# One attention kernel, eight batches: the last query projection a unit later, picks around the first scores, one key stack on GpSimd's queue

## The reference

```python
h = relu(layernorm(x))
q, k, v = h @ Wq.T + bq, h @ Wk.T + bk, h @ Wv.T + bv      # split into 8 heads of 32
scores = einsum('bhqd,bhkd->bhqk', q, k) * 32 ** -0.5
scores = scores * (adj + adj)[:, None]                     # 1024 x 1024 per head
attn = softmax(scores, axis=-1)
x = x + einsum('bhqk,bhkd->bhqd', attn, v) @ Wo.T + bo
```

## Time and profile before

| | us |
|---|---|
| median of 3 runs (lowest to highest) | 3013.35 (3013.23 to 3013.98) |
| the profiled execution's own time | 3014.05 |
| its span, first to last instruction | 3012.2 |
| TensorE matmuls busy | 2938.3 (98%) |
| VectorE busy | 1873.0 (62%) |
| ScalarE busy | 1492.1 (50%) |
| GpSimd busy | 702.0 (23%) |

### The profile page before, as it was taken

One profiled execution on the slowest core, in us unless ns is written; L12 is line 12 of the kernel. 1 busy time (PEld: TensorE's weight loads), 2 busy tenths in 40 slices (PEclk: granted clock), 3 DMA queues, 4 the chain that ended last, 5 costly groups with the idle time before them and its releaser, 6 DMA issues.

```text
span 3012.2 us, 63662 instructions
## 1 busy us (share of the span) xinstructions
PE 2938.3 (98%) x23040; PEld 2370.1 (79%) x23040; DVE 1873.0 (62%) x4154; ACT 1492.1 (50%) x2761; POOL 702.0 (23%) x1273
## 2 busy tenths in 40 slices
PE   7999999999999999999999999999999999999999
PEld 6787787877878778788787887888868888688886
DVE  2798427984278742787428874288643886438863
ACT  1784217833178332782328732287323873238722
POOL 0343003430034201242013420134201341013410
PEclk9999999999999999999999999999999999999999
DMA  5202212022120221202311113111121112220200
GB/s 173 92 2 92 78 71 92 2 92 79 70 92 2 92 106 52 84 14 80 132 36 73 41 53 133 48 59 58 56 113 70 38 70 68 89 81 26 82 8 14
DMA packets 96344, 204.34 MB, mean 68 GB/s; under 512 B 10512, under 2 KB 41616, under 8 KB 96016
## 3 DMA queue, kind: packets, MB, share of 16 engines
q1 hardware_dynamic: 96016, 199.96, 18.3%
HBM read 136.75 MB, written 8.65 MB: 48 GB/s over the span
## 4 chain that ended last, share of the span: by engine, by line
PE 72%; issue 10%; DVE 9%; POOL 4%; ACT 3%; SPq 1%; DVEq 0%; DMA 0%; POOLq 0%; ACTq 0%
PE ps L1113 40%; PE ps L1364 10%; PE ps L1289 8%; PE ps L1267 4%; PE ps L1436 4%; PE ps L1317 4%; POOL H L575 3%; DVE Z L803 2%; DVE stats L626 1%; DVE junk L845 1%; DVE h L861 1%; PE ps L1150 1%; POOL nm L563 1%; ACT Z L1038 1%; ACT h2T L1069 1%
## 5 line engine op out<-in xcount | busy, mean ns | idle before, releaser
L803 DVE CUSTOM_DVE_ANT_0 Z<-ps,adjN 128x1024 f32<-128x1024 f32 x512 | 623.6, 1218 | 66.2 <-PE ps L1267 66.2
L1038 ACT ACTIVATE Z<-Z,nm 128x1024 f32<-128x1024 f32 x512 | 587.1, 1147 | 72.2 <-POOL nm L563 72.2
L1289 PE MATMUL ps<-ident,Z 128*128 128x128 f32 x4096 | 546.4, 276 | 26.5 <-ACT Z L1038 17.6
L1289 PEld LDWEIGHTS ps<-ident,Z 128*128 128x128 f32 x4096 | 458.1, 140 | 138.8 <-issue 63.7
L1267 PE MATMUL ps<-kS,qS 128*128 128x512 f32 x1024 | 370.6, 444 | 4.5 <-ACT kS L1015 3.4
L575 POOL TENSOR_SCALAR H<-adjN 128x128 fp32r<-128x128 f32 (+1 forms) x456 | 316.8, 695 | 0.0
L563 POOL TENSOR_TENSOR nm<-nm,minus 128x1 f32<-128x1 f32 x512 | 97.1, 190 | 704.5 <-DVE nm L803 700.0
L1113 PE MATMUL ps<-mh,adjT 128*128 128x256 f32 x1024 | 224.8, 380 | 0.0
L1113 PE MATMUL ps<-v,P 128*128 128x257 f32 x1024 | 223.6, 379 | 0.0
L1113 PE MATMUL ps<-hT,t3T 128*128 128x512 f32 x512 | 221.0, 592 | 0.0
L1113 PEld LDWEIGHTS ps<-v,P 128*128 128x128 f32 x1024 | 193.8, 189 | 31.9 <-issue 3.8
(11 more groups left out here) (177 smaller groups left out, 5687.7 us busy)
## 6 DMA issues: line engine op xcount, KB each, us to landing
adjT<-adjT_in SPq DMA_DIRECT2D x8, 4096.0 KB, 13.0
adjN<-adj_in SPq DMA_DIRECT2D x8, 4096.0 KB, 17.8
adjT<-adjT_in SPq DMA_DIRECT2D x8, 2048.0 KB, 7.8
qS<-qhi SPq DMA_DIRECT2D x112, 128.0 KB, 2.1
qS<-qlo SPq DMA_DIRECT2D x112, 128.0 KB, 2.1
adjT<-adjT_in SPq DMA_DIRECT2D x8, 1536.0 KB, 11.9
xn<-x_in SPq DMA_DIRECT2D x8, 1024.0 KB, 6.1
kS<-khi SPq DMA_DIRECT2D x64, 128.0 KB, 2.1
```

The lines of the kernel that those rows point to most:

```text
L803: dve.tensor_tensor_reduce(Z[:, u % ZS], ps[:, 2 * (u % 2):2 * (u % 2) + 2].rearrange("p a n -> p (a n)"), adjN[:, u // HEADS], SCORE_SCAL ...
L1038: act.activation(Z[:, u % ZS], Z[:, u % ZS], ACT.Exp, bias=nm[:, u:u + 1], accum_out=sm[:, u:u + 1]).then_inc(exps.sem, 1)
L1289: mm = pe.transpose(ps[:, turn_bank((u, s)), rows(a)], Z[:, u % ZS, rows(NT // 2 * s + a)], ident[:])
```

## The change

Five edits, all of the same start of attention: VectorE's lower part of projection 7 goes from iteration 3 to iteration 4; ScalarE's upper part of it goes from the end of iteration 2 to iteration 3, between `exp(3)` and `evacuate(2)`; the six picks are ordered so that the three that head 3 needs come first, and the sixth is issued after `scores(0)`, which waits for three copies rather than five; and the stack of keys (1,1) leaves SP's queue for GpSimd's, ahead of its loop over units. TensorE's own place for projection 7 stays.

```diff
-    LASTS = ((0, 0, 0, 4, 1), (1, 0, 0, 5, 3), (0, 1, 0, 6, 4), (1, 1, 0, 7, 4), (0, 0, 1, 4, 5), (0, 1, 1, 5, 6))
+    LASTS = ((0, 0, 0, 4, 1), (1, 0, 0, 5, 3), (0, 0, 1, 6, 5), (1, 1, 0, 7, 5), (0, 1, 0, 4, 5), (0, 1, 1, 5, 6))
...
+        def stack(queue, dst, parts, j, cols, done):
+
+            for r, src in enumerate(parts):
+                to = dst[r:P:HPG].rearrange("p (g j) n -> p g j n", j=HPG)[:, :, j, cols]
+                queue.dma_start(to.bitcast(F32), src[j:P:HPG, :, cols].bitcast(F32)).then_inc(done.sem, 16)
...
                 stack_k(1, 0)
                 stack_q(0, 1)
-                stack_k(1, 1)
-                stack(kS, (khi, khi, klo, klo), HPG - 2, slice(0, N), kS_in[0][HPG - 2])
+                stack(sp, kS, (khi, khi, klo, klo), HPG - 2, slice(0, N), kS_in[0][HPG - 2])
                 stack_q(0, 2)
...
                 pool.tensor_tensor(x[:], x[:], bo1B[:].unsqueeze(1).broadcast_to([P, NT, D]), ALU.add).then_inc(xbo.sem, 1)
+                pool.wait_ge(*lo_s(b, 6))
+                stand(pool, waited_pool)
+                stack(pool, kS, (khi, khi, klo, klo), 1, half(1), kS_in[1][1])
...
                     if u == 1:
                         lower_kq(KQ_FIRST)
-                    if u - 1 in BESIDE and BESIDE[u - 1][0] == "q":
-                        lower_kq(BESIDE[u - 1][1])
+                    if u - 2 in BESIDE and BESIDE[u - 2][0] == "q":
+                        lower_kq(BESIDE[u - 2][1])
...
+                    if u - 1 in BESIDE and BESIDE[u - 1][0] == "q":
+                        upper_kq(BESIDE[u - 1][1])
                     if 1 <= u < UNITS + 1:
                         evacuate(u - 1)
                     if u == 0:
                         upper_kq(KQ_FIRST)
                         copy_v(0)
-                    if u in BESIDE:
-                        what, n = BESIDE[u]
-                        copy_v(n) if what == "v" else upper_kq(n)
+                    if u in BESIDE and BESIDE[u][0] == "v":
+                        copy_v(BESIDE[u][1])
...
-                for n, (w, g, s, at, split) in enumerate(LASTS):
+                def pick_last(n):
+                    w, g, s, at, split = LASTS[n]
                     pe.wait_ge(*lo_s(b, split))
                     if n >= 4:
                         pe.wait_ge(*lasts(b, n - 3))
...
-                pe.wait_ge(*lasts(b, 5))
+                for n in range(len(LASTS) - 1):
+                    pick_last(n)
+                pe.wait_ge(*lasts(b, 3))
                 scores(0)
+                pick_last(len(LASTS) - 1)
                 project_kq(KQ_FIRST)
                 pe.wait_ge(*lasts(b, len(LASTS)))
                 scores(1)
```

More of the change, by code:

```diff
@@ L449, in batch @@
             def batch(b, last):
[L452 to L456, removed]
                 def stack_k(s, j):
-                    stack(kS, (khi, khi, klo, klo), j, half(s), kS_in[s][j])
+                    stack(sp, kS, (khi, khi, klo, klo), j, half(s), kS_in[s][j])
                 def stack_q(s, j):
-                    stack(qS, (qhi, qlo, qhi, qlo), j, half(s), qS_in[s][j])
+                    stack(sp, qS, (qhi, qlo, qhi, qlo), j, half(s), qS_in[s][j])
                 sp.wait_ge(*lo_s(b, 2))
```

## The result

The changed kernel takes 2997.61 us (median of 6 runs, 2995.89 to 3000.65) against 3013.29 us before (6 runs, 3010.86 to 3014.16): ratio 0.995, 95% interval 0.994 to 0.996. That is 15.7 us less; 16.2 were forecast. A later run of the same kernel gave 2998.06 (5 runs) against 3013.14 on its chip. The profiled execution of after has a span of 2995.7 us.

The account below looks back on a forecast made before the run. TensorE was taken to bound the kernel, with 72% of the chain of waits. 1.78 us per batch, 14.2 over eight, plus 1.98 made 16.2 us off 3013.35: 2997.15 us, range 2994 to 3013.

Parts of the forecast that it names:

- Step 1: Reordered picks: scores 0 start 0.95 us earlier, less the sixth pick behind them; 0.45 us per batch taken.
- Step 2: Projection 7's parts a unit later: transposes 3 gain 0.98 us, scores 6 another 0.35; 1.33 us per batch.
- 0.3 us of margin: Time left between evacuate(2) freeing its bank, about 1.5 us after transposes 2, and transposes 3's second half at 1.86.
- Step 3: Keys (1,1) off SP's queue: scores 4 stop waiting, 1.98 us in all; queries (0,2) land in time for scores 6.
- Step 4: The same four DMAs on GpSimd, ahead of negate_max(0): up to 1.03 us each, so no cost.
- The deadline: Latest start of the first maximum's sign on GpSimd, 97.27, so that transposes 0 are not late.
- the free time: GpSimd's time for four DMAs before the first sign is due: 4.12 us, 1.03 us each.
- (a): GpSimd's DMAs hold it 1.03 to 1.5 us each; at 1.3 it costs 8.6 us, time 3005.8; chance 0.25.
- (b): GpSimd takes over 1.53 us per DMA, making the change slower than before; 3031 at 2.1 us; chance 0.15.
- (c): A DMA wait returns at scores 4 or 6, two queues sharing engines; 1.1 us per batch, 3006; chance 0.06.
- (d): Transposes 3's gap returns as a wait for ScalarE or VectorE; 0.4 to 1.3 us per batch, 3001 to 3007; chance 0.06.

Follow-up runs that it names:

- e5: Changed kernel with ScalarE's upper part of projection 7 back at the end of iteration 2, ahead of exp(3); 3003.81 us, ratio 0.9969.
- e5b: Changed kernel with VectorE's lower part of projection 7 back in iteration 3, ahead of evacuate(1) and Z(4); 3008.64 us, ratio 0.9988.
- e4: Changed kernel with the stack of keys (1,1) left on SP's queue, so only picks and projection 7 changed; 3007.55 us, ratio 0.9981.
- e6: Changed kernel with GpSimd's stack cut into eight DMAs of 64 KB instead of four of 128 KB; 3004.47 us, ratio 0.9974.
- e7: Changed kernel with GpSimd's four DMAs behind the first sign of a maximum instead of ahead of it; 2996.44 us, ratio 0.9945.
- e10: The changed kernel itself measured again, unaltered, on the chip of two later variants; 2998.06 us.

## Why the prediction was right, point by point

The forecast was 2997.2 us, measured were 2997.61; its terms, from the distances:

| step | forecast | measured |
|---|---|---|
| 1, picks, per batch | 0.45 | 0.51 (3.57 + 4.48 against 2.59 + 4.95) |
| 2, transposes 2 to 3 | 0.98 | 0.98 |
| 2, transposes 3 to scores 6 | 0.35 | 0.35 |
| 3, transposes 1 to scores 4, all batches | 1.98 | 1.98 |
| 4, GpSimd | 0 | 0 |
| a new wait | 0 | 0.97 in one batch |
| sum over all | 16.2 | 15.7 |

**Step 1** was right in mechanism. Scores 0 came 0.98 us earlier (0.95), and the new wait of the third pick for the fifth lower part shows as 0.20 us of idle weight loads. It costs nothing, since the copies are paced by ScalarE: the third starts 1.93 us after the first pick before and after (93.18 - 91.25, 91.66 - 89.73).

**Step 2** was right, and with the 0.3 us of margin that I gave, in another order. The upper part started not 0.20 but 0.38 us after transposes 2 (104.32 - 103.94), because exp(3) came first, and evacuate(2) ended at 1.55 instead of about 1.5, against 1.86. VectorE's lower part ended at 1.85 (105.04 + 0.75 - 103.94) instead of 1.7, well ahead of 2.70. exp(3) ended at 0.40 (103.19 + 1.15 - 103.94), forecast was about 0.5. e5 and e5b show that each engine's half was needed.

**Step 3** said that without it a new DMA wait of 1.1 us per batch would eat most of step 2. e4 measures this: 9.9 us more than the changed kernel, or 1.2 per batch. It named scores 6 as the place. In fact most of it stands already at scores 4, with 1.74 to 2.06 us from transposes 1; where scores 4 have waited, scores 6 hardly do.

**Step 4** was right in sum and off in its parts. GpSimd's DMAs start not at 93.15 in the old frame, 1.90 us after the first pick, but 2.46 to 2.51 us after it (92.24 - 89.73, 461.81 - 459.35). That is 0.65 us after the lower part they wait for has ended in batch 0 (VectorE's two last lower parts start at 89.97 and take 1.62) and 0.59 in batch 1, a start-up that I had not counted. The deadline was 6.02 us after the first pick (97.27 - 91.25); e6, whose sign at 7.04 made transposes 0 1.02 us late, gives the same. So the free time was 3.5 us, 0.88 for each DMA, not 1.03. The hold was 0.59 to 0.62 each, the lower bound, and 1.0 to 1.2 us per batch stay unused. My mark for this step, the sign straight behind `Z(0)` and not behind a DMA, is met in time (0.09 us behind the maximum in batch 1) but not in order: the row ahead of the sign is a DMA in every batch, and in batches 0 and 7 it makes the sign 0.18 and 0.08 us later than in e7. Of the Trainium skill's two rules, the first-byte latency of about 1 us ("DMA: Bandwidth & Descriptors", Latency and other measured facts) did not hold the engine: 0.59 to 0.62 us per issue was measured. The "DVE blocks DMA" trap ("SBUF — State Buffer", in the section on its two separate sides) was not put to the test: the pair of DMAs from 93.60 ran beside `Z(0)` (93.24 to 94.47), which reads PSUM, in 1.10 us, against 1.23 to 1.36 for the pair ahead of it.

**The rivals.** (a) and (b) fell since one DMA holds GpSimd for 0.6 us and not for over 1.03; that a longer hold would have been paid by TensorE is what e6 shows. (c), a DMA wait that returns, happened in one batch of the first trace, at scores 2 and not at scores 4 or 6, for 0.97 us instead of 8.8. Its mechanism, two queues at work at once, shows in the landings; over five traces it cost 0.7 to 1.4 us in five of 40 batches. (d) didn't happen.

**Where luck helped.** The sum is closer than its parts. Step 1 gave 0.5 us more in all than forecast, the new wait took 1.0, and beyond transposes 6 each batch gives back about 0.1 us in the changed kernel (345.8 us to the next first pick before, 345.9 after), 0.7 in all. In e10, without that wait, the distances gain 16.8 us and the medians 15.1. So each step is confirmed by its own distance, and the agreement of the total within half a microsecond is in part luck.

What stays open: why each batch gives back that 0.1 us. And the 1.5 us between traces at the program's start are unexplained.

## What to carry to other kernels

An instruction that waits is paid for by what is queued behind it. Follow the released wait on every engine at once: here ScalarE's queue would have kept 0.8 of 1.0 us, and SP's queue two thirds of the whole gain (e4 against the changed kernel), though the releaser in the trace named VectorE alone. Edits to one chain don't add: parts worth 0.4, 5.3 and 2.3 us alone were 15.7 together, so a part that shows nothing by itself is no reason to drop it. After such a repair read the next gap in the same way; the copy ahead of exp(6) was the same pattern, and worth another 6 to 8 us.

## What the runs showed of the hardware

- A DMA within SBUF of 64 rows, issued by GpSimd, held that engine for 0.55 to 0.57 us, the first of four for 0.67 (0.80 in batch 0), with rows of 2 KB or 1 KB alike (four of 128 KB in 2.34 us, eight of 64 KB in 4.55). SP's issue of the same transfer takes 0.60 us in the median and now and then far more, up to 1.98 in the kernel before and 2.30 in the changed one.
- The first of them starts 0.59 to 0.65 us after the work it waits for has ended, though without a wait ahead of it (e7) it starts within 0.13 us of the sign's start. SP's first DMA behind the eighth lower part starts 0.09 us after that has ended (105.88 against 105.04 + 0.75, the changed kernel, batch 0).
- Its landing takes 2.5 to 2.8 us in the median against 2.1 for SP's. While both queues are at work, SP's landings of keys (1,0) `khi` take 2.4 to 3.8 us (two traces of the changed kernel, medians of two), where the kernel before has 2.0 to 2.7, and `klo` had 4.8 for one in batch 2. The longest of them, 3.8, comes with a slow issue: in batch 7 SP's pair is held for 2.95 us after and for 2.47 before.
